# Attention outputs of a decoder layer: the multiply by the reciprocals on GpSimd instead of VectorE

## The reference

```
x = layernorm(x + self_attention(x))        # softmax((q k^T + q rel_k) / sqrt(8)) (v + rel_v)
x = layernorm(x + cross_attention(x, ctx))  # causal over 128 tokens
x = layernorm(x + moe_ffn(x))               # 8 experts, top 2 by the router, one shared expert, GELU
```

## Time and profile before

| | |
|---|---|
| median of 3 runs | 451.35 us (451.09 to 451.75) |
| the profiled execution, its own time | 451.89 us |
| its span, from the first to the last instruction | 450.1 us |
| mean granted TensorE clock | 0.942 of full speed |
| PE busy | 378.3 us, 84% of the span |
| DVE busy | 303.4 us, 67% |
| ACT busy | 228.3 us, 51% |
| POOL busy | 80.0 us, 18% |

### The profile page before, as it was taken

The page is one execution under the profiler, slowest core; times in us unless marked ns, Lnnn a source line. Parts: engine busy times, 40 slices in busy tenths (PEclk is TensorE's granted clock), DMA queues, the critical chain, the costliest instruction groups (busy, mean ns, idle before and its releaser), DMA issues.

```text
span 450.1 us, 11284 instructions
## 1 busy us (share of the span) xinstructions
PE 378.3 (84%) x4714; PEld 285.1 (63%) x4729; DVE 303.4 (67%) x630; ACT 228.3 (51%) x329; POOL 80.0 (18%) x92
## 2 busy tenths in 40 slices
PE   2556366974789999999999999999998989899992
PEld 1345234763566797767687976776685757566672
DVE  4246984469987679998775889998549476056324
ACT  2343046560069875326877853469944315844330
POOL 8910000020044012011131120003311202411001
PEclk9987559996989999999999999999999999999997
DMA  3261028724101360400112703010200310000100
GB/s 93 73 183 39 4 51 248 202 71 128 28 4 41 108 178 1 128 4 4 39 39 82 214 4 106 4 37 4 75 3 2 100 31 6 1 1 0 25 1 23
DMA packets 29420, 26.87 MB, mean 60 GB/s; under 512 B 12673, under 2 KB 27962, under 8 KB 28602
## 3 DMA queue, kind: packets, MB, share of 16 engines
q1 hardware_dynamic: 26042, 25.86, 20.7%
q10 hardware_dynamic: 3136, 0.27, 0.5%
q0 software_dynamic: 192, 0.03, 0.0%
HBM read 18.38 MB, written 7.35 MB: 57 GB/s over the span
## 4 chain that ended last, share of the span: by engine, by line
PE 54%; DVE 17%; DMA 10%; issue 6%; ACT 5%; SPq 5%; POOL 1%; POOLq 0%; DVEq 0%; ACTq 0%
PE ps_f L725 9%; PE ps_s L547 9%; PE ps_f L714 8%; PE ps_f L573 6%; PE ps_f L581 4%; DMA parts_by_head<-part 3%; PE ps_f L677 3%; PE ps_f L520 3%; DMA QS<-parts_by_head 3%; DVE ST L943 3%; PE ps_s L540 3%; DVE MX L946 3%; PE ps_s L556 2%; PE ps_f L526 2%; PE ps_s L636 2%
## 5 line engine op out<-in xcount | busy, mean ns | idle before, releaser
L547 PE MATMUL ps_s<-QS,KS 125*128 125x128 bf16 (+1 forms) x768 | 79.5, 249 | 11.9 <-DVE ST L943 6.6
L547 PEld LDWEIGHTS ps_s<-QS,KS 125*128 125x128 bf16 (+1 forms) x768 | 65.1, 106 | 34.6 <-DVE ST L943 9.0
L846 ACT ACTIVATE HT<-ps_f,hb 128x512 f32<-128x512 f32 x72 | 48.3, 688 | 74.0 <-PE ps_f L714 44.3
L725 PEld LDWEIGHTS ps_f<-w,HT 128*128 128x128 f32 x576 | 68.8, 192 | 8.1 <-issue 6.0
L725 PE MATMUL ps_f<-w,HT 128*128 128x128 f32 x576 | 72.1, 276 | 0.1
L714 PE MATMUL ps_f<-x2T,w 128*128 128x512 f32 x144 | 70.8, 602 | 1.4 <-DVE acc L1056 1.0
L488 POOL TENSOR_SCALAR_AFFINE_SELECT PC<-PC 128x1024 f32<-128x1024 f32 x32 | 34.8, 1094 | 142.2 <-ACT PC L810 142.2
L1060 DVE SCALAR_TENSOR_TENSOR acc<-ps_f,gw,acc 128x128 f32<-128x128 f32 x128 | 35.7, 341 | 21.8 <-PE ps_f L725 21.5
L810 ACT ACTIVATE PC<-ps_s 128x1024 f32<-128x1024 f32 x32 | 32.2, 1024 | 33.4 <-PE ps_s L547 30.1
L803 ACT ACTIVATE ST<-ST 128x1024 f32<-128x1024 f32 x32 | 33.9, 1061 | 28.0 <-DVE ST L974 27.6
L943 DVE TENSOR_TENSOR ST<-ps_s,ST 128x1024 f32<-128x1024 f32 x32 | 38.6, 1207 | 11.0 <-PE ps_s L547 10.9
(11 more groups left out here) (118 smaller groups left out, 525.2 us busy)
## 6 DMA issues: line engine op xcount, KB each, us to landing
parts_by_head<-part SPq DMA_DIRECT2D x16, 384.0 KB, 2.6
QS<-parts_by_head SPq DMA_DIRECT2D x24, 256.0 KB, 3.8
KS<-parts_by_head SPq DMA_DIRECT2D x24, 256.0 KB, 4.3
xin<-in_x SPq DMA_DIRECT2D x16, 64.0 KB, 2.7
cin<-in_ctx SPq DMA_DIRECT2D x4, 256.0 KB, 5.0
w<-in_L_ffn_rw SPq DMA_DIRECT2D x1, 1024.0 KB
out_x<-acc SPq DMA_DIRECT2D x16, 64.0 KB, 1.8
QS<-MP SPq DMA_DIRECT2D x32, 8.0 KB, 2.1
```

Source lines behind the costliest of these rows:

```text
L547: last = nc.tensor.matmul(ps[:, o:o + S], KS[a][0:kd, c:c + S], queries(a, kd, h, j), start=not masked and j == 0, stop=j == NB - 1, skip_ ...
L725: last = nc.tensor.matmul(ps[:, b * E:(b + 1) * E], HT[n % 2][:, f, b * S:(b + 1) * S], w2[:, e, f, :], start=f == 0, stop=f == NF - 1 and ...
L846: nc.scalar.activation(HT[n % 2][:, f, :], ps[:, :], ACT.Gelu, bias=hb[:, e, f:f + 1]).then_inc(ht_ready, 1)
```

## The change

On DVE the steps `X` and `cX` keep the reciprocal and lose the multiply with the wait ahead of it. On POOL a new branch does the multiply, in the steps `XT` and `cXT`: it waits for the reciprocal, and for the last normalisation that stands ahead of it in the order, since that reads `Y`. It reports on the same semaphore `X_ready[a]`, which PE and ACT wait for as before.

```diff
@@ GpSimd's loop
+                elif what in ("XT", "cXT"):
+
+                    a = int(what == "cXT")
+                    g.wait_ge(rl_ready[a], ch + 1)
+                    normal = [u for u in ORDER[:ORDER.index((ch, what, t))] if u[1] in ("ln", "cln")]
+                    if normal:
+                        g.wait_ge(ln_ready[int(normal[-1][1] == "cln")], normal[-1][0] + 1)
+                    den = X[a][:, :, :, HD:HD + 1]
+                    nc.gpsimd.tensor_tensor(Y[:, :, :].rearrange("p b (h d) -> p b h d", h=H), X[a][:, :, :, 0:HD],
+                                            den.broadcast_to([P, NB, H, HD]), ALU.mult).then_inc(X_ready[a], 1)
@@ VectorE's loop
                     den = X[a][:, :, :, HD:HD + 1]
                     nc.vector.reciprocal(den, den).then_inc(rl_ready[a], 1)
-                    v.wait_ge(rl_ready[a], ch + 1)
-                    nc.vector.tensor_tensor(Y[:, :, :].rearrange("p b (h d) -> p b h d", h=H), X[a][:, :, :, 0:HD], den.broadcast_to([P, NB, H, HD]), ALU.mult).then_inc(X_ready[a], 1)
```

## The result

The changed kernel takes 453.64 us (median of 6 runs, 452.41 to 455.22) against 451.02 us for the kernel before (6 runs, 449.59 to 451.75): 1.0066 times the time before, with a 95% interval of 1.0038 to 1.0094, so 3.0 us slower by the ratio and 2.6 by the medians. Forecast were 4.5 us, as 455.8 us in a range of 453.2 to 461.0. The sign and the wide range held; the size came out at two thirds. One execution of the kernel before in a later comparison took 925.36 us, twice the usual time, and is left out of the ratio there.

A forecast was written before the change was run, and what follows sets the result against it. TensorE's full, in-order queue was taken to bound the kernel. Waits of 0.5 + 0 + 0.39 + 0.15 + 0.37 + 0.05 + 0.54 + 2.49 = 4.5 us, added to 451.35, gave 455.8 us, range 453.2 to 461.0.

The forecast's parts named there:

- What bounds: Whole kernel: TensorE's queue is full and in order, so each late `Y` moves everything behind it unless another engine is later.
- The price of a multiply on GpSimd: Each moved multiply: 1.27 us, taken from GpSimd's bias add; bounded by 0.69 us below and 2.55 us above.
- The step rule: GpSimd's read of heads 36 bytes apart: if steps above 8 bytes counted, 1.70 us per multiply, sum some 2.9 us larger.
- The handoff: Between reciprocal and multiply: GpSimd starts 0.05 us after the reciprocal, so TensorE can load `Y` 1.37 us after the old start.
- The eighth place: At `1cXT`: the multiply waits on GpSimd behind `fln`'s small adds and power, making TensorE's load 2.49 us late.
- The lock at `1cXT`: The multiply holds up VectorE's normalisation of `acc` by 0.94 us, 2.06 instead of 1.12, and no one waits for it.
- The seven plain places: The `XT` and `cXT` steps other than `1cXT`: losses of 0.5, 0, 0.39, 0.15, 0.37, 0.05 and 0.54 us.
- Slow patterns: Rival, chance 0.17: GpSimd's multiply is dearer, 1.9 us, giving about 460.2 us; at 2.55 some 465.
- The normalisation goes first: Rival, chance 0.11: at `1cXT` VectorE's four normalisations go ahead and the multiply waits their 1.12 us, giving 456.9 us.
- TensorE recovers the big wait: Rival, chance 0.12: the 2.5 us at `1cXT` is made good later in waits for query DMAs, giving 453.4 us.

The follow-up runs named there:

- eight forms: Changed kernel with eight different 128 x 512 sums and products replacing GpSimd's eight multiplies; forms took 1.04 to 1.29 us, 365.9 us from `0X` to the end.

## Why the prediction was right, and where its size was off

- *What bounds.* Held in the main: 1.0199 with seven multiplies 1.04 us later, and 1.0006 with all left out, so VectorE's relief is worth about 1.2 of 5.5 us at most and perhaps nothing. That each late `Y` is lost was too strong: of 1.15 and 1.16 us at `2X` and `3X` little appears behind them. By its own measure (a load within 1.0 us of the multiply's end) it also held for eight places and not seven, with 0.98 us at `0cX`. And the full queue was read at `1cXT` alone; in the twelve microseconds from 96 us on, behind `0X`, TensorE is busy for 6.27.
- *The price of a multiply on GpSimd.* This is the main term that was mis-sized: 1.04 us, not 1.27. By the prediction's own steps `Y` comes 1.14 us after the old multiply's start instead of 1.37, so all eight places shrink by 0.23: `0XT` about 0.3, `1XT` 0.16, `2cXT` 0.14, `3cXT` 0.31, `2XT` and `3XT` together some 0.1, `1cXT` 2.26. That sum is 3.3 us instead of 4.5, and 3.0 were measured by the ratio (interval 1.7 to 4.2), 2.0 and 2.4 in the two pairs of profiles from `0X` on. The shares given to the single plain places are finer than any of these numbers can test. "The same operation class, type and size" was the wrong way to pick the row: sum or product did not matter and the pattern did; size was not varied. The bounds of 0.69 and 2.55 did hold it.
- *The step rule.* A multiply of 1.70 us, as the rule of the Trainium skill ("GPSIMD Engine Reference", section "Performance pitfalls for Q7 kernels") on reads with a step above 8 bytes would have it if it counted here, was not seen. The remedy that the Trainium skill gives there speaks of the inner step, and here that is 4 bytes, since the eight numbers of a head are adjacent; the 36 bytes between heads are an outer step. The form with it was the cheapest of all, 1.04 us. None of the eight forms has an inner step above 8 bytes.
- *The handoff.* GpSimd starts 0.08 us after the reciprocal's end, where VectorE started 0.03 after it. The sum had put it 0.05 us behind VectorE's old start, and that is what it was.
- *The eighth place.* The order of events was as forecast: `fln`'s statistics start earlier, by 0.72 us against 0.61, the power ends, the multiply follows, and TensorE is 2.06 us late against 2.49. 0.23 of the difference is the multiply's price, 0.11 the statistics' earlier start, and the rest small steps between them. In the kernel with eight forms a product of 1.27 us stood there, and TensorE loaded 4.37 us after the reciprocal's start, 2.28 later than before. The place was forecast as 55% of the loss; alone it cost 1.0055, some four fifths of the whole, and put ahead of `fln` it gave back two thirds.
- *The lock at `1cXT`.* As forecast the multiply went first and the normalisation took 1.83 us, 0.71 more than before (0.94 were forecast, from an add of 1.27 us). No one waited for it. VectorE was busy for 299.3 us and not 298, of which this is 0.7. The trace agrees with the rule of the Trainium skill ("SBUF — State Buffer", section "SBUF: two separate sides") that whichever starts first holds the shared ports: the multiply was in front by 0.06 us, and the first normalisation ended 0.08 us after it.
- *The seven plain places.* 2.0 us were forecast for them, about 1.0 with the right price, and 0.6 measured (interval from -0.3 to 1.5).
- *The rivals.* "Slow patterns" had the wrong sign. "The normalisation goes first" did not happen in either profile of after. "TensorE recovers the big wait" came closest to the measured median, 453.4 against 453.64, and looked right in the first pair of profiles; it is refuted by the kernel that has that wait alone, at 1.0055 (interval from 1.0031). That its number was close is chance: a multiply of 1.04 us made the loss smaller, and nothing was recovered.

## What to carry to other kernels

Work that is moved to an idle engine takes its place in that engine's queue, and there it can stand behind something that waits for a third engine; here one such word of eight made most of the loss, and two thirds of it went away when the multiply was put ahead of that word. Busy shares say nothing of it: GpSimd was 18% busy. Before moving work away from an engine, leave it out once: if the time does not fall, the move has nothing to win. And look at what the kernel without it does in its place: here a fill of 0.48 us hid part of what such a run is to show.

## What was not expected

- GpSimd's time for the same 128 x 512 elements depends on the access pattern, not on sum or product: 1.28 us with two plain tensors, 1.16 with the second operand standing still over eight elements, 1.04 with that and `X`'s layout.
- 7.8 us of lateness in seven places cost 9.0 by the ratio, of which 6.9 stand behind the first of them in the profile, and unevenly: double at `0X`, next to nothing at `3X`. TensorE's granted clock was 0.86 over the stretch with the first long wait, against 1.00.
- Profiles of the same code differ in a stretch by more than the effect that is sought: by 1.3 to 1.6 us from `0X` to `1cX`, by some 3 us ahead of `0X`. Two profiles of before differ by 0.3 us from `2X` to `2cX`, where the wait for one DMA differs by as much, and the first pair of profiles suggested a recovery by it that did not exist. A profile of a third kernel was worth more than a second look at the two.
